# Routing six tiles ahead of the expert stream, 79 expert tiles per image instead of 80, and eleven output buffers

## The chip, the cores and the metric

The kernel runs on one core of one Trainium2 chip. The metric is the device time of one execution in microseconds. A core has TensorE (PE), VectorE (DVE), ScalarE (ACT), GpSimd (POOL) and SyncE (SP, which here only issues DMAs), each with its own in-order instruction stream; they meet at semaphores. SP, ACT and POOL start transfers, which 16 DMA engines carry out.

## The reference, cut to what matters

```python
# x: (2, 256, 96, 96)
x = x + conv_ref(_ln_c(x), ...)       # 4 dilated softmax branches, projection, group norm, relu
t = _to_tokens(x)                     # 2 * 9216 tokens of 256 channels
t = t + _L0_ffn_ref(_ln_t(t), ...)    # the mixture of experts below
x = _from_tokens(t, x)

def _moe(tokens, router_w, w1, b1, w2, b2):      # 8 experts, top 2
    probs = softmax(tokens @ router_w.T)
    rw, re = top_k(probs, 2);  rw = rw / rw.sum(-1)
    combine = zeros(N, 8).at[arange(N), re].set(rw)
    out = tokens
    for e in range(8):
        h = gelu(tokens @ w1[e] + b1[e], approximate=False)
        out = out + combine[:, e:e+1] * (h @ w2[e] + b2[e])
    return out
```

## The kernel before, in words

The program first does the convolution of image 0 and then that of image 1, up to about 1377 us. The routing of image 0 is done beside the convolution of image 1. What the change touches comes after it: the **expert stream**, which runs from 1377 us to 2145 us, and then the outputs of image 1.

**Expert tiles.** Each of an image's 9216 tokens goes to two experts, so there are 18,432 rows of 256 floats. The rows of one expert lie together in DRAM (`expert_in`), and the stream takes them 256 at a time. Each expert's last tile may be partly filled. `ETILES` is 18432 / 256 + 8 = 80 tiles per image, `STREAM` 160. For a tile SP loads `e_x` (`load_tile`, three buffers), PE turns it (`turn_in`), ACT and DVE split it (`e_hi`, `e_lo`), PE multiplies by the first weights (`first_product`, 12 matmuls), ACT applies gelu and splits (`hidden`, `e_act`, `h_hi`), DVE makes `h_lo`, PE multiplies by the second weights (`second_product`, 12 matmuls), DVE adds a bias into `e_out` (`output`), and POOL scatters `e_out` to DRAM (`expert_out`) by row indices with two indirect DMAs (`send`). `e_out` has `EO` = 4 buffers. Before the stream DMAs bring the first weights' second part (2.5 MB) and the second weights (`w2`, 4 MB).

**Routing of image 1.** It is interleaved with the stream of image 0. A tile iteration `n` has four ticks, `4n` to `4n + 3`; `routing(1, tick)` on each engine does what its `Schedule` has for that tick. A *slot* is one tile of 128 tokens: ACT loads blocks of two tiles (`load_block`) and applies relu (`relu_block`), DVE adds (`add_block`), PE turns the tile and makes the logits (`turn_tile`), ACT keeps them in `r_ln` (`keep_slot`), DVE takes the moments. Six slots are a *pair* (72 slots, 12 pairs). After a pair's last slot come its standard deviation, the choice of two experts in some twenty small DVE operations (`choose`), residual and normalisation of its six tiles, and, after ranking on PE at slot `RANK_AT`, the places of its rows (`place`). POOL then scatters them to `expert_in` with 12 indirect DMAs in three thirds of four (`scatter_rows`); `scatter_after` says behind which tile's `send` each third stands. `r_ln` has buffers for `HELD` = 3 pairs: ACT's first slot of pair p waits for the scatters of pair p - 3. Slots stand 3.5 ticks apart from tick 12 on, so 8 slots go with 7 tiles, from tile 3 to tile 65. After pair 11 DVE builds the tables of image 1 (`tables`); SP then writes fill rows behind each expert's rows (`fill_ends`, 8 DMAs at the first tile of image 1), waits for those and for all row scatters, and loads that tile.

**Outputs.** While the stream of image 1 runs, image 0 is finished in 24 groups of 384 tokens: ACT loads `o_y` (768 KB) and `o_acc` (384 KB), DVE weighs, PE turns, ACT copies and stores 384 KB. `out_group_at` puts one group on every third tile from tile 87 to 156. The 24 groups of image 1 follow after the stream.

## Time and profile before

| | us |
|---|---|
| median of three runs | 2252.12 (2251.94 to 2254.53) |
| the profiled execution, its own time | 2248.74 |
| span of its profile | 2246.9 |
| convolution, to | about 1377 |
| expert stream | 1377 to 2145 |
| outputs of image 1 | 2145 to 2247 |

| engine | busy us | share |
|---|---|---|
| PE | 1910.4 | 85% |
| DVE | 1560.9 | 69% |
| ACT | 1333.7 | 59% |
| POOL | 1083.1 | 48% |

The profiled execution took 3.4 us less than the median. Its own time is 1.8 us more than its span. Where this text says tile n it is the n-th expert tile from 0, and its time is the start of the DVE instruction that writes its `e_out`. The clock column is the TensorE clock granted, as a share of 2.4 GHz.

### The profile page before, as it was taken

To read this page: it belongs to the slowest core of one execution; us is meant where nothing else is said; L and a number is where in the kernel's file an instruction comes from. 1 tells how busy PE (TensorE), PEld (TensorE's weight loads), DVE (VectorE), ACT (ScalarE), POOL (GpSimd) and SP (SyncE) were. 2 spreads that over 40 slices of the span, in tenths; PEclk is the share of its full clock that TensorE was granted. 3 is DMA by queue.
4 is the path that set the end of the run, shared out by engine and by line. 5 is a ranking of instruction groups with operands and counts; after the bars stand their busy time and mean duration, and the time that the engine had idled before them with its cause. 6 is when DMAs were issued, how large, how long until landed. Compare 5 with 4: busy or idle time off the path is not lost.

```text
span 2246.9 us, 56560 instructions
## 1 busy us (share of the span) xinstructions
PE 1910.4 (85%) x20204; PEld 1832.1 (82%) x20204; DVE 1560.9 (69%) x4184; ACT 1333.7 (59%) x2877; POOL 1083.1 (48%) x1430
## 2 busy tenths in 40 slices
PE   5899799999969997999998895888888868999943
PEld 4899798999859997898888884888887768999932
DVE  4577675666556775777777774688887856777765
ACT  4677343333327774556556541887777758888822
POOL 3666212222215663145655562367777775555510
PEclk9999799999979998999999997898899989999965
DMA  4332597567554434677888879567667667888889
GB/s 143 105 106 78 145 294 189 141 173 174 153 142 133 132 102 111 190 228 216 227 232 245 237 209 322 171 219 227 224 218 225 202 192 274 284 282 283 280 310 368
DMA packets 341802, 459.87 MB, mean 205 GB/s; under 512 B 82677, under 2 KB 262709, under 8 KB 339173
## 3 DMA queue, kind: packets, MB, share of 16 engines
q1 hardware_dynamic: 231208, 246.52, 38.7%
q10 hardware_dynamic: 68433, 109.55, 14.9%
q0 software_dynamic: 41888, 100.18, 13.0%
q8 instruction: 168, 2.75, 0.5%
q14 instruction: 105, 0.86, 0.1%
HBM read 291.86 MB, written 174.69 MB: 208 GB/s over the span
## 4 chain that ended last, share of the span: by engine, by line
PE 46%; ACT 14%; DVE 13%; POOL 9%; issue 7%; DMA 7%; ACTq 3%; SPq 1%; POOLq 1%; DVEq 1%
PE ps_y L424 17%; PE ps_a L424 7%; PE ps_o L1050 6%; PE ps_b L987 4%; POOL expert_in L2148 4%; PE ps L424 3%; ACT w_now L1494 3%; POOL expert_out L2224 3%; ACT e_act L1483 3%; DMA o_acc<-res_scratch 3%; PE ps_tok L897 1%; DVE cat_lo L1938 1%; PE ps_o L1037 1%; ACT h_hi L1486 1%; DMA y_scratch<-y_acc 1%
## 5 line engine op out<-in xcount | busy, mean ns | idle before, releaser
L424 PE MATMUL ps_y<-cat_hi,wp 128*128 128x288 f32 x2048 | 483.5, 312 | 1.8 <-DVE cat_lo L1938 1.8
L2224 POOL DMA_INDIRECT expert_out<-e_out,e_dest x320 | 327.4, 1023 | 248.2 <-DVE e_out L2048 177.2
L2202 POOL DMA_DIRECT2D patches<-rows_scratch x340 | 190.4, 604 | 499.3 <-PE ps_o L1037 301.4
L424 PEld LDWEIGHTS ps_y<-cat_hi,wp 128*128 128x128 f32 x2048 | 354.4, 195 | 2.0 <-DVE cat_lo L1938 2.0
L2148 POOL DMA_INDIRECT expert_in<-r_ln,r_pos x288 | 290.0, 1007 | 106.3 <-issue 86.3
L2168 POOL TENSOR_TENSOR taps<-taps,g_rows 96x108 f32<-96x108 f32 (+2 forms) x416 | 243.8, 611 | 162.5 <-ACT g_rows L1310 158.6
L1379 ACT ACTIVATE bands<-ps_b 112x288 f16<-112x288 f32 (+4 forms) x256 | 105.1, 411 | 345.4 <-PE ps_b L987 331.9
L424 PE MATMUL ps_y<-cat_lo,wp 128*128 128x288 f32 x1024 | 308.1, 301 | 0.0
L424 PE MATMUL ps<-w,h_hi 128*128 x1280 | 258.5, 301 | 53.9 <-DVE h_lo L2037 51.1
L1938 DVE SCALAR_TENSOR_TENSOR cat_lo<-ps_o,cat_hi 128x288 fp32r<-128x288 f32 (+1 forms) x576 | 228.2, 419 | 92.9 <-ACT cat_hi L1385 89.4
L424 PE MATMUL ps<-e_hi,w_now 128*128 128x256 f32 x1280 | 266.1, 292 | 4.8 <-ACT w_now L1494 2.1
L1385 ACT ACTIVATE cat_hi<-ps_o 128x288 fp32r<-128x288 f32 (+1 forms) x576 | 211.9, 384 | 97.5 <-PE ps_o L1037 49.6
L424 PEld LDWEIGHTS ps<-w,h_hi 128*128 128x128 f32 x1280 | 206.0, 199 | 68.7 <-issue 68.2
L1930 DVE SCALAR_TENSOR_TENSOR bands<-ps_b,bands 112x288 f16<-112x288 f32 (+4 forms) x256 | 116.5, 455 | 189.1 <-ACT bands L1379 182.3
L1050 PE MATMUL ps_o<-bands,patches 112*128 112x72 f16 (+2 forms) x4608 | 198.4, 201 | 40.3 <-DVE cat_lo L1938 24.9
L424 PEld LDWEIGHTS ps<-e_hi,w_now 128*128 128x128 f32 x1280 | 218.1, 199 | 6.4 <-issue 4.0
L1050 PEld LDWEIGHTS ps_o<-bands,patches 112*128 112x128 f16 (+2 forms) x4608 | 176.9, 102 | 48.0 <-issue 46.5
L424 PEld LDWEIGHTS ps_y<-cat_lo,wp 128*128 128x128 f32 x1024 | 200.0, 195 | 0.0
L1483 ACT ACTIVATE e_act<-ps,b_of 128x256 f32<-128x256 f32 x320 | 133.9, 471 | 109.5 <-PE ps L424 70.6
L424 PE MATMUL ps_a<-wg,xc_hi 128*96 128x324 f32 x768 | 180.1, 320 | 11.6 <-DVE xc_lo L1902 11.6
L424 PE MATMUL ps<-e_lo,w_now 128*128 128x256 f32 x640 | 184.6, 288 | 0.0
L424 PE MATMUL ps<-w,h_lo 128*128 x640 | 184.4, 288 | 0.0
(201 smaller groups left out, 4488.3 us busy)
## 6 DMA issues: line engine op xcount, KB each, us to landing
e_x<-expert_in SPq DMA_DIRECT2D x160, 260.0 KB
patches<-rows_scratch SPq DMA_DIRECT2D x160, 192.0 KB
patches<-rows_scratch SPq DMA_DIRECT2D x256, 108.0 KB
patches<-rows_scratch SPq DMA_DIRECT2D x204, 112.0 KB
x_in<-in_x SPq DMA_DIRECT2D x48, 384.0 KB, 3.7
rows_scratch<-rows_st SPq DMA_DIRECT2D x48, 384.0 KB, 4.2
r_x<-in_x ACTq DMA_DIRECT2D x72, 256.0 KB
r_y<-y_scratch ACTq DMA_DIRECT2D x72, 256.0 KB
```

What stands on the lines that cost most here:

```text
L424: mm = eng.matmul(out, lhs[p], rhs[q], start=start and n == 0, stop=stop and n == 2)
L987: return pe.matmul(out, sel[:, b, 3 * y + x], pixels, start=True, stop=True, skip_group_check=True)
L1050: mm = pe.matmul(out, ring[:, (2 * p + z) * C + c * 128:(2 * p + z) * C + (c + 1) * 128], band_of[:, q, p * 72:(p + 1) * 72], start=k == 0 ...
L1379: act.activation(bands[0:k, s % 2, 0, first:first + n], ps_b[0:k, 0:n], ACT.Relu).then_inc(band_hi_done, 1)
L1385: act.activation(cat_pixels(cat_hi[:, s % 2, c], s, j), out_pixels(ps_o[:, n % 2], s), ACT.Copy, scale=UNSCALE).then_inc(cat_hi_done, 1)
L1483: last = act.activation(e_act[:, u, f], ps_1[:, u, f], ACT.Gelu, bias=b1_of[:, r, f, i:i + 1])
L1930: dve.scalar_tensor_tensor(out=bands[0:k, s % 2, 1, first:first + n], in0=ps_b[0:k, 0:n], scalar=0.0, in1=bands[0:k, s % 2, 0, first:first ...
L1938: dve.scalar_tensor_tensor(out=cat_pixels(cat_lo[:, s % 2, c], s, j), in0=out_pixels(ps_o[:, n % 2], s), scalar=UNSCALE, in1=cat_pixels(ca ...
L2148: pool.indirect_dma_start(out=xs_dram, out_offset=bass.IndirectOffsetOnAxis(ap=r_pos[:, p % HELD, z, t:t + 1], axis=0), in_=r_ln[:, p % HE ...
L2168: last = pool.tensor_tensor(here, here, g_rows[:, u, first:end, i, b:b + nb].rearrange("p r b k -> p r (b k)"), ALU.add)
L2202: pool.dma_start(patch_target(s, n), patch_source(m, s, n)).then_inc(patch_pooled[s % RING], 16)
L2224: pool.indirect_dma_start(out=ys_dram, out_offset=bass.IndirectOffsetOnAxis(ap=e_dest[:, i, j:j + 1], axis=0), in_=e_out[:, u, j], in_offs ...
```

## The change

One expert tile per image is left out: 7 experts at most can have a partly filled tile beyond 72 full ones, so 79 always suffice. `ETABLE` keeps 80 entries in the tables, `ETILES` is 79, `STREAM` 158. Then: slots stand 4 ticks apart and begin at tick -24, so that six slots are done before tile 0 and one goes with each tile up to 65; the group norm of image 1 stands ahead of them, and the load of `w2` behind the first two block loads; `group_factors(1)` and the first two `add_block` of DVE move ahead in the same way. `e_out` gets seven more buffers (`e_more`), in a ring of eleven up to tile 142 (`SHORT` = 143) and of four after it. Row scatters stand up to five tiles earlier in POOL's stream than the slots' plan alone would have them. Output groups stand 2.65 tiles apart, from tile 93 to 154. `send(n)` now waits for the scatters of tile n - 4.

```diff
-ETILES = PIX * TOP // S + E
+ETABLE = PIX * TOP // S + E
+ETILES = ETABLE - 1
+EO_MORE = 7
...
-        RANK_AT = TP + 4
-        SLOTS = RANK_AT + TP * (CPAIRS - 1) + 1
+        RANK_AT = (TP + 4, TP + 2)
+        SLOTS = [at_ + TP * (CPAIRS - 1) + 1 for at_ in RANK_AT]
+        AHEAD = 24
-        expert_ticks = [4 * 3 + (7 * k_ + 1) // 2 for k_ in range(SLOTS)]
+        expert_ticks = [4 * k_ - AHEAD for k_ in range(SLOTS[1])]
...
-        OUT_FIRST = ETILES + 7
+        OUT_RING = EO + EO_MORE
+        SHORT = (STREAM - 2 * EARLY - 4) // OUT_RING * OUT_RING
+        def out_buffer(n):
+            u = n % OUT_RING if n < SHORT else (n - SHORT) % EO
+            return e_out[:, u] if u < EO else e_more[:, u - EO]
+        def out_user_before(n):
+            return n - OUT_RING if n < SHORT + EO else n - EO
+        def sent_through(n):
+            return 16 * (S // 128) * (n // EO + 1)
+        OUT_FIRST = ETILES + 14
+        OUT_LAST = STREAM - 4
+        out_tile = {OUT_FIRST + g_ * (OUT_LAST - OUT_FIRST) // (GROUPS_OUT - 1): g_ for g_ in range(GROUPS_OUT)}
...
+            pe.wait_ge(r_kept, slots_before(1, 0))
+            group_sums(1, ps_g)
             turn_in(0)
             turn_in(1)
+            for u in range(-AHEAD, 0):
+                routing(1, u)
...
-            act.wait_ge(tabled, TABLE_ALL)
-            input_hi(0)
-            input_hi(1)
-            act.wait_ge(w_loaded_1, 32)
-            weights_hi(0)
-            weights_hi(1)
+            group_deviation(1)
             act.wait_ge(y_stored, 16 * (24 + 18))
             act.wait_ge(y_pooled, 16 * 6)
             for j in range(RY):
                 load_block(BLOCKS + j)
+            act.dma_start(w2[:].rearrange("p e z c -> p (e z c)").bitcast(F32), w_dram[1].rearrange("p e z c -> p (e z c)")).then_inc(w_loaded_2, 16)
+            act.wait_ge(tabled, TABLE_ALL)
+            input_hi(0)
+            input_hi(1)
+            act.wait_ge(gn_dve, 18)
+            for j in range(RY):
+                relu_block(BLOCKS + j)
+            load_block(BLOCKS + RY)
+            for u in range(-AHEAD, 0):
+                routing(1, u)
+            act.wait_ge(w_loaded_1, 32)
+            weights_hi(0)
+            weights_hi(1)
...
-                after(dve, e_scattered[n % EO], 16 * (S // 128) * (n // EO))
+                used = out_user_before(n)
+                if used >= 0:
+                    dve.wait_ge(e_scattered[used % EO], sent_through(used))
...
             def send(n):
+                if n >= EO:
+                    pool.wait_ge(e_scattered[u], sent_through(n - EO))
                 pool.wait_ge(e_out_done, n + 1)
...
             def scatter_after(p, q):
-                return plans[1].placed(p) // 4 - 1 + q
+                return plans[1].placed(p) // 4 - 1 + q - (OUT_RING - EO - 1) * p // CPAIRS
```

How ACT's stream reads from the load of the first weights' second part on (`w` is either weights tile, 128x8192 is `w2`), first before:

```order
L1468 DMA w<-expert_weights 128x5120 [waits proj_done]
L1470 DMA w<-expert_weights 128x8192
L1475 ACTIVATE e_hi<-ps_x 128x512 [waits e_turned,tabled]
L1475 ACTIVATE e_hi<-ps_x 128x512 [waits e_turned]
L1492 TENSOR_LOAD etable [waits w_loaded_1]
L1492 ISA x2
L1494 ISA
L1494 ACTIVATE w_now<-w 128x1024
```

and then the same place of the changed kernel:

```order
L1497 DMA w<-expert_weights 128x5120 [waits proj_done]
L1231 ACTIVATE gn_tmp<-gn_tmp,eps 128x2 [waits gn_dve]
L1239 DMA r_x<-in_x 128x2x256 [waits r_tok,r_x1,y_pooled,y_stored]
L1240 DMA r_y<-y_scratch 128x2x256
L1239 DMA r_x<-in_x 128x2x256 [waits r_x1,r_tok]
L1240 DMA r_y<-y_scratch 128x2x256
L1563 DMA w<-expert_weights 128x8192
L1503 ACTIVATE e_hi<-ps_x 128x512 [waits e_turned,tabled]
L1503 ACTIVATE e_hi<-ps_x 128x512 [waits e_turned]
L1247 ACTIVATE r_y<-r_y,gn_bias,gn_scale 128x256 [waits r_loaded0,gn_dve]
```

The load of `w2` moved behind the wait for `y_stored` and two block loads, and in front of all later block loads.

POOL's stream at the end of the routing, first before (the last two pairs' thirds among the scatters of the tiles; x2 is one tile):

```order
L2148 DMA expert_in<-r_ln,r_pos 155648x260 x4
L2224 DMA expert_out<-e_out,e_dest 45056x256 x6
L2148 DMA expert_in<-r_ln,r_pos 155648x260 x4
L2224 DMA expert_out<-e_out,e_dest 45056x256 x2
L2148 DMA expert_in<-r_ln,r_pos 155648x260 x4
L2224 DMA expert_out<-e_out,e_dest 45056x256 x2
L2148 DMA expert_in<-r_ln,r_pos 155648x260 x4
L2224 DMA expert_out<-e_out,e_dest 45056x256 x176
```

and of the changed kernel:

```order
L2180 DMA expert_in<-r_ln,r_pos 155648x260 x4
L2258 DMA expert_out<-e_more,e_dest 45056x256 x8
L2180 DMA expert_in<-r_ln,r_pos 155648x260 x4
L2258 DMA expert_out<-e_more,e_dest 45056x256 x2
L2180 DMA expert_in<-r_ln,r_pos 155648x260 x4
L2258 DMA expert_out<-e_more,e_dest 45056x256 x2
L2180 DMA expert_in<-r_ln,r_pos 155648x260 x4
L2258 DMA expert_out<-e_out,e_dest 45056x256 x8
```

Before, 88 tiles' scatters stand behind the last row scatter, so 72 stand ahead of it. Now the last three thirds stand behind the scatters of tiles 63, 64 and 65, so 66 tiles stand ahead.

## Rows read from the trace of the kernel before

**Rows 1.** The page's first line.
```profile
span 2246.9 us, 56560 instructions
```

**Rows 2.** Windows: stretch, length, busy time of each engine, clock, DMA share, GB/s.
```profile
1377.00:1406.50 29.50, 2.23 (x8) 1.45 (x9) 8.19 (x19) 2.39 (x4) 5.39 (x6) 0.54 0.96 388
1406.50:1435.00 28.50, 24.48 (x170) 22.73 (x171) 17.72 (x40) 23.54 (x40) 6.18 (x6) 0.88 0.59 181
...
1480.00:1780.00 300.00, 249.66 (x1936) 239.53 (x1935) 249.73 (x790) 236.49 (x442) 229.91 (x225) 0.91 0.69 223
1780.00:1850.00 70.00, 48.43 (x366) 46.52 (x367) 44.39 (x112) 38.76 (x67) 54.04 (x53) 0.88 0.60 191
...
1900.00:2145.00 245.00, 233.91 (x1979) 227.57 (x1978) 184.48 (x394) 201.13 (x350) 134.46 (x134) 1.00 0.83 277
2145.00:2247.00 102.00, 36.51 (x144) 27.43 (x144) 59.46 (x145) 19.47 (x24) 3.19 (x4) 0.51 0.94 358
```

**Rows 3.** DMA issues from 1376 to 1420: kind, count, size, median us to landing.
```profile
w<-expert_weights ACTq DMA_DIRECT2D x1, 4096.0 KB, 25.4
...
y_scratch<-y_acc POOLq DMA_DIRECT2D x6, 384.0 KB, 22.9
...
b<-in_b ACTq DMA_DIRECT2D x1, 1024.0 KB, 6.8
```

**Rows 4.** Timeline of PE, the start: us, duration, line, tiles, idle before and releaser.
```profile
1397.38 1.11 PE L1113 MATMUL ps_x<-ident,e_x 128*128 128x128 f32 x4 [20.79 <-DMA e_x<-expert_in]
...
1406.51 0.55 PE L424 MATMUL ps<-e_hi,w_now 128*128 128x256 f32 x1 [2.12 <-ACT w_now L1494]
```

**Rows 5.** Timeline of DVE: the e_out of tiles 0, 65, 77, 83, 92, 159.
```profile
1421.82 0.69 DVE L2048 TENSOR_TENSOR e_out<-ps,b 128x512 f32<-128x512 f32 x1 [0.29 <-PE ps L424]
...
1777.43 0.69 DVE L2048 TENSOR_TENSOR e_out<-ps,b 128x512 f32<-128x512 f32 x1 [0.81 <-PE ps L424]
...
1843.09 0.68 DVE L2048 TENSOR_TENSOR e_out<-ps,b 128x512 f32<-128x512 f32 x1
...
1863.03 0.69 DVE L2048 TENSOR_TENSOR e_out<-ps,b 128x512 f32<-128x512 f32 x1
...
1899.98 0.68 DVE L2048 TENSOR_TENSOR e_out<-ps,b 128x512 f32<-128x512 f32 x1
...
2145.20 0.69 DVE L2048 TENSOR_TENSOR e_out<-ps,b 128x512 f32<-128x512 f32 x1 [1.23 <-PE ps L424]
```

**Rows 6.** Groups by line, POOL, 1480 to 1780.
```profile
L2148 POOL DMA_INDIRECT expert_in<-r_ln,r_pos x120 | 121.3, 1011 | 36.6 <-issue 36.6
...
L2224 POOL DMA_INDIRECT expert_out<-e_out,e_dest x105 | 108.9, 1037 | 33.6 <-issue 30.2 <-DVE e_out L2048 3.5
```

**Rows 7.** Groups by line, DVE, 1480 to 1780: the part of one routed tile.
```profile
L1632 DVE BATCH_NORM_STATS2 r_stats<-r_ln 128x6 f32<-128x256 f32 x60 | 25.0, 417 | 0.0
...
L1634 DVE BATCH_NORM_AGGREGATE r_mv<-r_stats 128x2 f32<-128x6 f32 x60 | 10.9, 182 | 2.1
...
L1624 DVE TENSOR_TENSOR r_x<-r_x,r_y 128x512 f32<-128x512 f32 x28 | 19.1, 683 | 0.0
```

**Rows 8.** Waits: ACT from 1480 to 1780, then DVE from 1800 to 1850.
```profile
ACT r_ln L1231 <- DMA expert_in<-r_ln,r_pos: 9.7, 3, 5.8
...
DVE e_out L2048 <- DMA expert_out<-e_out,e_dest: 20.1, 6, 6.5
```

**Rows 9.** Timeline of SP, POOL and PE, 1813 to 1839: the hand-over.
```profile
1813.79 10.50 SPq L780 DMA_DIRECT2D expert_in<-in_k_fill  x8
...
1831.78 0.96 POOL L2148 DMA_INDIRECT expert_in<-r_ln,r_pos  x1 [0.30 <-issue]
...
1838.03 1.11 PE L1113 MATMUL ps_x<-ident,e_x 128*128 128x128 f32 x4 [8.13 <-DMA e_x<-expert_in]
```

**Rows 10.** From 1900 to 2100: waits of PE, groups of POOL.
```profile
PE ps_x L1113 <- DMA e_x<-expert_in: 0.3, 1, 0.3
...
L2224 POOL DMA_INDIRECT expert_out<-e_out,e_dest x107 | 108.0, 1009 | 92.2 <-DVE e_out L2048 73.1 <-issue 19.1
```

More of the change, by code:

```diff
@@ L322, in build @@
         o_out = sbuf(ctx, "o_out", [128, 2, CC, TC])
+        with ExitStack() as r1:
+            e_more = sbuf(r1, "e_more", [128, EO_MORE, S // 128, C])
         res_early = sbuf(ctx, "res_early", [128, EARLY, TT, C])
@@ L529, in __init__ @@
                 self.pair_end = {self.ticks[TP * p + TP - 1]: p for p in range(CPAIRS)}
-                self.pair_rank = {self.ticks[TP * p + RANK_AT]: p for p in range(CPAIRS)}
+                self.pair_rank = {self.ticks[TP * p + rank_at]: p for p in range(CPAIRS)}
             def kept(self, p, h):
@@ L535, in placed, with ranked_in @@
             def placed(self, p):
-                return max(self.ticks[TP * p + RANK_AT] + 4, self.ticks[TP * p + TP - 1] + 17)
-        plans = (Schedule(conv_ticks, (-2, 2), (-1, 1)), Schedule(expert_ticks, (-3, 1), (-3, 3)))
-        def ranked_in(k):
-            return (k - RANK_AT) // TP if k >= RANK_AT and (k - RANK_AT) % TP == 0 else None
+                return max(self.ticks[TP * p + self.rank_at] + 4, self.ticks[TP * p + TP - 1] + 17)
+        plans = (Schedule(conv_ticks, RANK_AT[0], (-2, 2), (-1, 1)), Schedule(expert_ticks, RANK_AT[1], (-3, 1), (-3, 3)))
+        def ranked_in(r, k):
+            return (k - RANK_AT[r]) // TP if k >= RANK_AT[r] and (k - RANK_AT[r]) % TP == 0 else None
         def slots_before(r, k):
-            return r * SLOTS_KEPT + sum(i < ITILES or ranked_in(i) is not None for i in range(k))
-        SLOTS_KEPT = sum(i < ITILES or ranked_in(i) is not None for i in range(SLOTS))
+            kept_in = lambda q, end: sum(i < ITILES or ranked_in(q, i) is not None for i in range(end))
+            return sum(kept_in(q, SLOTS[q]) for q in range(r)) + (kept_in(r, k) if k else 0)
         ALL_PAIRS, ALL_BLOCKS = IMAGES * CPAIRS, IMAGES * BLOCKS
@@ L563, in out_loads, with sent_all @@
             return 16 * sum(1 if early(k) else 2 for k in range(g % OB, g + 1, OB))
-        OUT_FIRST = ETILES + 7
+        OUT_RING = EO + EO_MORE
[10 more added lines that the diff above has]
+        out_tile = {OUT_FIRST + g_ * (OUT_LAST - OUT_FIRST) // (GROUPS_OUT - 1): g_ for g_ in range(GROUPS_OUT)}
         GATE_AT = 20
         def out_group_at(n):
-            g = (n - OUT_FIRST) // 3
-            return g if n >= OUT_FIRST and (n - OUT_FIRST) % 3 == 0 and g < GROUPS_OUT else None
+            return out_tile.get(n)
+        def sent_all(u, tiles):
+            return 16 * (S // 128) * len(range(u, tiles, EO))
         def halves(s):
@@ L818, in _ @@
                 if n == STREAM - 2 * EARLY:
+                    for u in range(EO):
+                        sp.wait_ge(e_scattered[u], sent_all(u, SHORT))
                     for u in range(2):
@@ L1572, in _ @@
                     write_out(g)
-                if n >= OUT_FIRST - 3 and sent < GROUPS_OUT and sent <= (n - OUT_FIRST + 3) // 3 + OB - 2:
+                begun = sum(n_ <= n + 3 for n_ in out_tile)
+                if n >= OUT_FIRST - 3 and sent < GROUPS_OUT and sent <= begun + OB - 3:
                     load_outputs(sent)
@@ L2101, in _ @@
             dve.memset(r_ln[:, 1, :, MARK:XC], 0.0)
-            group_factors(1, ps_g)
+            for j in range(RY):
+                add_block(BLOCKS + j)
+            for u in range(-AHEAD, 0):
+                routing(1, u)
             for n in range(STREAM):
                 hidden_lo(n)
-                if n == 2:
-                    add_block(BLOCKS)
-                    add_block(BLOCKS + 1)
                 routing(1, 4 * n)
@@ L2239, in _ @@
             for u in range(EO):
-                pool.wait_ge(e_scattered[u], 16 * (S // 128) * STREAM // EO)
+                pool.wait_ge(e_scattered[u], sent_all(u, STREAM))
 _INS = [
```

71 lines of the change are left out of this document (30 added, 41 removed).

## The prediction

> **What bounds the kernel now.** I read the windows first. Up to 1377 us nothing is changed. Between 1377 and 1406.5 us PE works 2.23 of 29.5 us, while the DMA engines are 96% busy: the machine waits for weights, for y_scratch and for the first expert tiles [rows 2 to 4]. From 1480 to 1780 us, tiles with routing, no engine is full: PE 83%, DVE 83%, ACT 79%, all in one chain from tile to tile. POOL is the exception. Its 225 scatters have 230 us of busy time, and 66.8 us of "issue" lie between them; together that is 1.333 us per scatter, and it waited only 3.5 us for e_out [rows 2, 6]. So POOL is just as fast as the tiles. What this costs stands in the waits: 9.7 us of ACT on r_ln (three pairs of rows held), and after 1800 us, 20.1 us of DVE on the four e_out buffers, when POOL had fallen behind [rows 8]. At the hand-over to image 1 the last row scatter starts at 1831.78 us, and PE had stood still for 8.13 us when tile 80 arrived at 1838.03 us [rows 9]. After that PE is 95% busy at full clock (1900 to 2145 us), and the outputs of image 1 end the span in 102 us on DMA engines 94% busy [rows 2].
>
> **The tiles' own pace.** From tile 77 to 83, without routing or outputs, 19.94 us for 6 tiles: 3.3 us [rows 5]. From tile 0 to 65: 355.6 us, of which 65 x 3.3 = 214.5 are the tiles, 9.7 the r_ln waits, and 131.4 the routing. That is 72 slots and the later work of 11 pairs. Of one pair I count 48% as slots: on DVE a slot is 0.417 + 0.182 + 0.683 / 2 = 0.94 us [rows 7], 5.6 for six, about half of what a pair costs. So 131.4 / (12 x 0.48 + 11 x 0.52) = 11.45 us per pair.
>
> **The change, part by part.**
>
> 1. Start. Before, the first product is at 1406.51 us and tile 0 is out at 1421.82 [rows 4, 5]. Now blocks must come first. Their wait is y_scratch, 22.9 us to landing beside the weights' loads [rows 3]. With w2's 4 MB moved behind them I take 10 to 15 us less, about 1394; the same weight at 388 GB/s [rows 2] is 10.8 us. Two block loads, relu and add give slot 0 at about 1401. Block 2 is issued behind w2 on ACT's queue and I take it to land at 1409; then four slots, with relu and loads of blocks 3 and 4 in turn on ACT, give the end of slot 5 at about 1420, relu 4 and the first weights at 1424. The group norm lies in DMA time, free. First product 1424, tile 0 out 11 us later, since table loads and group norm no longer stand in it: **1435, +13 us**. Bounds: 1425 if w2 does not delay block 2 and y_scratch is early; 1462 if each of five block loads took the 6.8 us of the bias load [rows 3] on the path.
>
> 2. Tiles 0 to 65. 66 slots are left in place of 72, so 11 slot parts and 11 later parts: 65 x 3.3 + 11 x 11.45 = 340.5 us, tile 65 at 1775.5, as before (1777.43 [rows 5]). Half a pair's work went to the start, the r_ln wait goes, since a pair's rows now leave four tiles before its buffer is wanted (before, under two).
>
> 3. Tiles 66 to 76. 11 x 3.3 + 6 us of pair 11 = 42.3: tile 76 at 1817.8. With eleven buffers the 20.1 us of DVE waits go [rows 8]. What is late next, three things:
>  - POOL: 66 tiles x 2 + 144 row scatters = 276 ahead of the last, against 288. It is continuous from tile 2 on (1445), so 272 x 1.333 = 363: 1808.
>  - the rows themselves: places of pair 11 at tile 69.25, about 1795; 16 scatters behind it, 21 us: 1816.
>  - SP's fills: issued when tile 76 has been taken, at about tile 72, 1775.5 + 6 x 3.3 + 6 + 3.3 = 1804.6, and 10.5 us long [rows 9]: 1815.
>  All three, with the 5.3 us that lay between the last row scatter's end (1832.74) and PE's first turn (1838.03) [rows 9], here 5.5, come to **1821.5** for the first tile of image 1, against 1838.03: **-16.5 us**. They lie within 13 us of each other, so a cheaper tile gains little more.
>
> 4. The rest. Before, 2145.20 - 1838.03 = 307.2 us for 82 iterations; now 81, without output work at 3.3 to 3.7 each: **-3.6 us**. One tile less in image 0 is already in 3.
>
> 5. Outputs of image 0: 24 groups over 61 tiles in place of 69. PE's and ACT's work per group is the same, so as a sum nothing. But bytes: 61 x 0.528 MB + 24 x 1.573 MB = 70.0 MB. Tiles 92 to 159 took 245.2 us [rows 5], 67 x 3.3 + 24 x 1.0, so this stage should now take 61 x 3.3 + 24 x 1.08 = 227 us: 308 GB/s, where 277 went at 83% busy [rows 2]. By that share it would be 92%. Between 0 (PE waited 0.3 us for e_x in 200 us [rows 10]) and 25.6 us (rival C) I take **+2**, near the row.
>
> 6. send's wait for tile n - 4: eight scatters, 10.7 us, lie between. Nothing; up to a few us if landing took as long. The tail is unchanged: 102 us.
>
> Sum: -16.5 - 3.6 + 2 = -18.1, where the +13 of the start lies inside the first term. Against the profiled execution (2248.74 us, 1.8 more than its span of 2246.9 [rows 1]) that is 2230.6. The median of the runs is 3.4 higher, so **2234 us**.
>
> **The skill on two places.** In rows 6 a scatter takes 1011 and 1037 ns with DVE 83% busy, in rows 10 1009 ns at 75%. The Trainium skill, SBUF — State Buffer, "SBUF: two separate sides", says that GpSimd cannot write descriptors while DVE runs an operation on both ports; its part "A bandwidth-pool intuition that's wrong" gives about 3.1 us in place of 0.62 for such a DMA. If each scatter were held like that, 272 of them would be an estimated 843 us; the trace bears out hardly 30 ns, so the sum goes by 1.333. The second is block 2 behind w2: rows 3 show 25.4 us for w2 behind another load, and nothing here shows two loads overtaking. The Trainium skill, DMA: Bandwidth & Descriptors, "Queues, rings and completion order", says descriptors of one issuer are taken in ring order; that speaks against the change, and by it the block waits for all of w2; without it the start would be 5 us earlier.
>
> **Rivals.**
>
> A. Faster. Routing laid at one slot per tile costs a pair 9 us, since bursts no longer meet two slots. Tile 76 would be at 1791, but POOL's 1808 and the 5.5 us hold: 1813.5, 8 less: 2226; with the start 8 us early as well 2218. For it: DVE has 17% idle in small waits. Against: the chain, not the load, makes the pace.
>
> B. POOL still the bound. At 1.40 us per scatter it ends at 1826, tile 79 at 1831.5, ten more: 2244. For it: single scatters of 1.4 to 1.6 us lie in the trace's mean of 1037 ns; against: that mean.
>
> C. Slower: the DMA engines bound the stage with image 0's outputs. At the 277 GB/s of rows 2, 70.0 MB take 252.7 us instead of 227: 2234 - 2 + 25.6 = 2257.6, slower. It decides from 278 GB/s downward. For it: 8% to 11% more bytes per time, a tile load only three deep, share 83% already. Against: 358 GB/s in the last window, and PE never waited.
>
> D. The ring and the order buy nothing, because the tiles' chain takes back what the waits leave: -3.6 and the start half repaid, 2250.
>
> **How the numbers follow.** Forecast 0.45 (own range 2224 to 2245), A 0.23, B 0.11, C 0.13, D 0.08. A measurement of this kernel tells 0.2%, 4.5 us: same is 2247.6 to 2256.6. Faster: forecast, A and nearly all of B, 0.78. Same: D and the edge of B, 0.09. Slower: C, 0.13. The range leaves out A's better half and C's worse: 2212 to 2256.
>
> **What would show it.** The first product near 1424 and tile 0 near 1435; ACT waiting once for r_x or r_y of block 2. No ACT wait on expert_in, no DVE wait on expert_out up to tile 76. Tile 65 within 5 us of 1776. Row scatters ending near 1816, and SP's fills ending at about the same time. The stage with outputs at about 305 GB/s and PE's waits for e_x under 5 us. I am wrong if tile 0 is past 1445, if a pair costs over 12.5 us, or if PE waits for e_x among the outputs.

## The result, and the profile after

The changed kernel took 2259.11 us median of 20 runs (2249.64 to 2267.75), the kernel before beside it 2251.19 (20 runs, 2240.59 to 2256.63); the ratio is 1.0046, 95% interval 1.0034 to 1.0058. It is slower by about 0.46%, where the forecast of 2234 us stood for a gain of 0.8%. The profiled executions are 2263.68 and 2248.74 us: 14.9 us apart, while the medians are 7.9 apart, since one lies above its median and the other below. To read the numbers further on: in the three first and in the last session of experiments the kernel before itself took 2524 to 2544 us, in another 2248; chip 15 showed both levels, so each kernel is compared only with what ran beside it.

The page's first line, against [rows 1]:

```profile
span 2261.8 us, 56526 instructions
```

The windows of the changed kernel, against [rows 2] (same columns):

```profile
1377.00:1406.50 29.50, 6.80 (x36) 5.62 (x36) 12.87 (x32) 2.35 (x5) 5.41 (x6) 0.60 0.87 320
1406.50:1435.00 28.50, 9.97 (x45) 9.47 (x46) 10.68 (x23) 8.71 (x17) 0.00 (x0) 0.50 0.69 253
1480.00:1780.00 300.00, 248.70 (x1986) 242.76 (x1986) 249.46 (x758) 238.27 (x443) 219.89 (x219) 0.90 0.68 218
1780.00:1850.00 70.00, 52.28 (x389) 50.37 (x388) 51.40 (x132) 42.04 (x72) 52.66 (x52) 0.86 0.62 199
1900.00:2145.00 245.00, 226.46 (x1903) 221.35 (x1901) 183.94 (x391) 198.30 (x338) 133.40 (x127) 0.99 0.87 295
```

The second line shows the later start: from 1406.5 to 1435 us PE was busy 9.97 us where it had been 24.48. Among the tiles, from 1480 to 1780 us, no engine is fuller than before. The stages, from the starts of DVE's `e_out` instructions and PE's last convolution product (us; "start" is from that product to tile 0, T is 79, before 80):

| | conv. end | start | tiles 0-65 | 65 to image 1's first | its tile 0 to 14 | 14 to last | after it | span |
|---|---|---|---|---|---|---|---|---|
| before | 1376.6 | 45.2 | 355.6 | 75.9 | 55.7 | 236.2 | 101.7 | 2246.9 |
| after | 1380.4 | 70.8 | 342.6 | 67.3 | 50.5 | 245.5 | 104.6 | 2261.8 |

**The start.** Timelines of the changed kernel; first ACT and DVE:

```profile
1401.24 0.39 ACTq L1239 DMA_DIRECT2D r_x<-in_x  x1
...
1405.14 1.08 ACT L1247 ACTIVATE r_y<-r_y,gn_bias,gn_scale 128x256 f32<-128x256 f32 x2
...
1406.26 0.82 DVE L1824 TENSOR_TENSOR bias_parts<-erank,order 128x640 f32<-128x640 f32 x1
...
1410.58 0.66 DVE L1653 TENSOR_TENSOR r_x<-r_x,r_y 128x512 f32<-128x512 f32 x1
...
1422.19 0.60 ACT L1247 ACTIVATE r_y<-r_y,gn_bias,gn_scale 128x256 f32<-128x256 f32 x1 [7.26 <-DMA r_y<-y_scratch]
```

then PE (the second of its lines begins tile 0's second product), against [rows 4], and DVE, with tiles 0 and 65, against [rows 5]:

```profile
1411.38 0.66 PE L874 MATMUL ps_k<-ident,r_x 128*128 128x128 f32 x2 [12.51 <-DVE r_x L1653]
...
1433.04 0.55 PE L428 MATMUL ps<-e_hi,w_now 128*128 128x256 f32 x1 [4.21 <-ACT w_now L1522]
...
1441.79 0.49 PE L428 MATMUL ps<-w,h_hi 128*128 x2
...
1447.36 0.21 DVE L1715 TENSOR_TENSOR r_either<-r_chosen 128x48 f16<-128x48 f32 x1
...
1451.23 0.69 DVE L2080 TENSOR_TENSOR e_out<-ps,b 128x512 f32<-128x512 f32 x1 [0.63 <-issue]
...
1793.80 0.69 DVE L2080 TENSOR_TENSOR e_more<-ps,b 128x512 f32<-128x512 f32 x1 [0.69 <-issue]
```

`y_scratch` was complete at 1401.2, when ACT issued the first block. Slot 0 then waited for `add_block`, which stood on DVE behind five instructions of `first_biases` (4.3 us); block 2, issued behind `w2` on ACT's queue at 1411.33, let ACT wait 7.26 us. PE had the second product of tile 0 done at about 1443.4 us, but its `e_out` stands in DVE's stream behind the choice of pair 0 and other routing work, with which DVE was busy from 1441.2 to 1450.6 us without a pause.

**The tiles.** Waits of the changed kernel: PE and POOL from 1500 to 1800 us, then DVE's on the scatters from 1500 to 1850 (us in total, times, longest):

```profile
PE ps_k L884 <- DVE r_either L1715: 39.7, 10, 4.7
...
POOL expert_in L2180 <- DVE r_ln L1760: 15.9, 5, 5.9
...
DVE e_more L2080 <- DMA expert_out<-e_out,e_dest: 1.6, 2, 1.0
DVE e_more L2080 <- DMA expert_out<-e_more,e_dest: 1.3, 2, 0.7
```

The 20.1 us of DVE waits on the buffers and ACT's 9.7 us [rows 8] are gone. In their place are two that the kernel before did not have: PE stands in the ranking product for the choice of experts (ranking comes at slot TP + 2 instead of TP + 4), and POOL in the moved row scatters for rows not yet written.

POOL's groups of the changed kernel from 1480 to 1780 us, against [rows 6]:

```profile
L2180 POOL DMA_INDIRECT expert_in<-r_ln,r_pos x112 | 113.2, 1011 | 45.9 <-issue 30.6 <-DVE r_ln L1760 12.9 <-DVE e_more L2080 1.5
L2258 POOL DMA_INDIRECT expert_out<-e_more,e_dest x69 | 69.0, 1000 | 21.7 <-issue 20.4 <-DVE e_more L2080 0.9 <-DVE e_out L2080 0.3
L2258 POOL DMA_INDIRECT expert_out<-e_out,e_dest x38 | 37.7, 993 | 11.6 <-issue 11.3 <-DVE e_out L2080 0.3
```

219 scatters against 225: POOL did less per time, 12.9 us of it waiting for `r_ln`.

**The hand-over**, timeline of SP, POOL and PE, against [rows 9]:

```profile
1829.36 0.57 SPq L806 DMA_DIRECT2D expert_in<-in_k_fill  x1
...
1832.90 0.97 POOL L2180 DMA_INDIRECT expert_in<-r_ln,r_pos  x1 [0.30 <-issue]
...
1843.58 0.35 SPq L819 DMA_DIRECT2D e_x<-expert_in  x1
...
1846.15 1.11 PE L1141 MATMUL ps_x<-ident,e_x 128*128 128x128 f32 x4 [7.38 <-DMA e_x<-expert_in]
```

The last row scatter ends at 1833.87, 1.1 us later than before. SP's fills begin 15.6 us later than before, go on for 9.8 us, and only 4.4 us behind them is image 1's first tile loaded.

Which of the two was awaited last can be read from SP's waits from 1750 to 1850 us, first before, then changed (L783 is the wait for the row scatters, L817 the first instruction behind all waits of `fill_ends`):

```profile
SPq L783 <- DMA expert_in<-r_ln,r_pos: 10.0, 1, 10.0
...
SPq L817 <- DMA expert_in<-in_k_fill: 3.6, 1, 3.6
```

Before, SP waited 10.0 us for the row scatters and loaded 2.6 us behind the last one. In the changed kernel it waited for the fills, and the load came 9.7 us behind the last row scatter. The fills are issued when tile 72 is under way (its `e_out` is at 1828.1 us), so here the late tiles set the hand-over, and POOL's rows came second.

**The outputs**, waits of PE and SP from 1900 to 2150 us, against [rows 10]:

```profile
PE ps_x L1141 <- DMA e_x<-expert_in: 11.9, 6, 5.1
...
SPq L848 <- DMA expert_out<-e_more,e_dest: 9.1, 1, 9.1
```

L848 is SP's wait for all scatters up to tile `SHORT` - 1 = 142, just before it reuses `e_more`'s place for residuals; the tile loads are queued behind it, and PE starves 5.1 us.

### The profile page after: what moved, and what is told of

It is laid out like the page before. It is cut to its first block, busy times and chain, and to the rows that moved or that the text cites. A ratio compares the mean times of both kernels' runs of the same rounds, so it can differ in the third digit from the quotient of the medians.

```text
span 2261.8 us, 56526 instructions
## 1 busy us (share of the span) xinstructions
PE 1907.8 (84%) x20148; PEld 1836.5 (81%) x20148; DVE 1564.8 (69%) x4176; ACT 1331.4 (59%) x2865; POOL 1077.6 (48%) x1426
## 3 DMA queue, kind: packets, MB, share of 16 engines
q0 software_dynamic: 41696, 99.65, 12.8%
## 4 chain that ended last, share of the span: by engine, by line
PE 49%; DVE 20%; DMA 10%; ACT 8%; issue 6%; POOL 3%; DVEq 2%; ACTq 1%; SPq 1%; POOLq 1%
PE ps_y L428 17%; PE ps_a L428 7%; PE ps L428 6%; PE ps_o L1078 6%; PE ps_b L1015 4%; DMA out<-o_out 3%; DMA e_x<-expert_in 2%; DVE h_lo L2067 2%; PE ps_tok L925 2%; DVE e_lo L2057 1%; DVE cat_lo L1967 1%; ACT e_act L1511 1%; PE ps_o L1065 1%; DVEq L2073 1%; DVE r_x L1653 1%
## 5 line engine op out<-in xcount | busy, mean ns | idle before, releaser
L428 PE MATMUL ps<-w,h_hi 128*128 x1264 | 259.5, 304 | 31.3 <-DVE h_lo L2067 29.1
L428 PE MATMUL ps<-e_hi,w_now 128*128 128x256 f32 x1264 | 255.0, 286 | 5.4 <-ACT w_now L1522 4.2
L2258 POOL DMA_INDIRECT expert_out<-e_more,e_dest x182 | 184.5, 1014 | 100.1 <-DVE e_more L2080 52.4
L428 PEld LDWEIGHTS ps<-e_hi,w_now 128*128 128x128 f32 x1264 | 212.6, 197 | 6.0 <-issue 4.3
L2258 POOL DMA_INDIRECT expert_out<-e_out,e_dest x134 | 138.7, 1035 | 148.0 <-DVE e_out L2080 113.8
```

The source lines that it names most:

```text
L428: mm = eng.matmul(out, lhs[p], rhs[q], start=start and n == 0, stop=stop and n == 2)
L2258: pool.indirect_dma_start(out=ys_dram, out_offset=bass.IndirectOffsetOnAxis(ap=e_dest[:, i, j:j + 1], axis=0), in_=out_buffer(n)[:, j], in ...
```

## Experiments

Columns as above; "ratio" is to the kernel before in the same session, with its 95% interval. e1 to e4 ran in one session and e5, the changed kernel again, in the next, together with e6 to e8; a stage of e1 to e4 is compared with e5's across the two. By the ratio e1, e3 and e4 lie within e5's interval, so what is read from them is the stage alone. At the slower level:

| | start | 0-65 | 65-img1 | 0-14 | 14-last | after | ratio |
|---|---|---|---|---|---|---|---|
| f1 before, again | 44.0 | 478.8 | 94.0 | 56.0 | 247.9 | 102.9 | 0.9999 (0.997-1.0029) |
| e5 changed | 69.4 | 546.2 | 92.5 | 52.5 | 253.6 | 103.2 | 1.0372 (1.03-1.0444) |
| e1 w2 last | 61.8 | 543.1 | 91.0 | 54.7 | 255.2 | 103.2 | 1.0325 (1.0292-1.0358) |
| e2 TP + 3 | 68.7 | 506.4 | 100.6 | 54.0 | 256.1 | 102.9 | 1.024 (1.0201-1.0279) |
| e3 SHORT 132 | 69.2 | 544.6 | 89.4 | 54.0 | 246.4 | 103.4 | 1.0332 (1.0296-1.0369) |
| e4 every 3rd | 68.9 | 550.1 | 90.2 | 58.5 | 254.6 | 102.5 | 1.0357 (1.032-1.0394) |
| e6 e1+e2+e3 | 63.0 | 513.6 | 100.4 | 54.8 | 246.1 | 103.1 | 1.0223 (1.0154-1.0291) |
| e7 none ahead | 43.0 | 499.4 | 111.8 | 54.4 | 255.7 | 102.9 | 1.0162 (1.0095-1.0229) |
| e8 TP + 4 | 69.0 | 470.8 | 104.1 | 53.6 | 253.0 | 102.9 | 1.0121 (1.0055-1.0187) |
| f2 four edits | 59.5 | 473.1 | 104.1 | 53.5 | 243.3 | 104.4 | 1.009 (1.0056-1.0124) |
| f3 and no shift | 59.9 | 456.4 | 89.5 | 55.4 | 245.4 | 102.3 | 0.9972 (0.9946-0.9998) |
| f4 ring, none ahead | 42.9 | 468.1 | 89.2 | 54.6 | 249.5 | 103.1 | 0.9962 (0.9936-0.9988) |
| h1 as f2 | 59.7 | 473.5 | 105.2 | 55.5 | 243.7 | 104.6 | 1.0084 (1.0056-1.0113) |
| h2 12 ahead | 50.8 | 523.2 | 86.8 | 53.9 | 248.8 | 102.9 | 1.0118 (1.0079-1.0156) |

At the level of the prediction (before: 2248.17 us, 29 runs):

| | start | 0-65 | 65-img1 | 0-14 | 14-last | after | median | ratio |
|---|---|---|---|---|---|---|---|---|
| g1 no shift only | 69.5 | 340.3 | 68.2 | 50.4 | 245.5 | 103.5 | 2259.04 | 1.0045 (1.0032-1.0058) |
| g2 12 ahead | 51.6 | 354.4 | 68.0 | 50.7 | 243.8 | 103.2 | 2246.16 | 0.9988 (0.9974-1.0003) |
| g3 24 ahead | 60.1 | 335.2 | 77.7 | 51.8 | 237.5 | 102.3 | 2248.38 | 1.0002 (0.9987-1.0017) |
| g4 no ring | 45.6 | 355.7 | 76.5 | 50.2 | 241.9 | 102.5 | 2250.55 | 1.001 (0.9997-1.0023) |

**e1, `w2` behind the slots.**

```diff
-            act.dma_start(w2[...] ...)      # behind the first two load_block
             for u in range(-AHEAD, 0):
                 routing(1, u)
+            act.dma_start(w2[...] ...)
             act.wait_ge(w_loaded_1, 32)
```

> The changed kernel with one edit: ACT issues the load of w2 (4 MB) after the six slots of the start instead of before the load of block 2. Theory S (the start eats the gain: in the changed kernel the first product came 52.6 us after the last projection, 29.9 before, and ACT waited 7.3 us for block 2 behind w2): the first product comes 5 to 8 us earlier (about 46 us), tile 0 follows 18 us behind it, and the run is 5 to 8 us faster than the changed kernel. Rival (hand-over fixed by something else, so that an earlier start is given back): first product earlier, but tile 65 to image 1's first tile (67.3 us) grows by as much and the time stays within 2 us. A second way to miss: w2 now lands after tile 0 needs it, then PE waits before the first second product and tile 0 comes over 22 us after the first product.

The start is 7.6 us shorter than e5's (51.2 to 43.6 us up to the first product), the rest as it was. ACT's wait for block 2, 7.26 us in the changed kernel, was `w2` ahead of it on the queue.

**e2, ranking one slot later**, and **e8, two slots later** (as before).

```diff
-        RANK_AT = (TP + 4, TP + 2)
+        RANK_AT = (TP + 4, TP + 3)          # e8: TP + 4
```

> The changed kernel with one edit: the ranking of a pair on PE one slot (four ticks) later, RANK_AT TP + 3 in place of TP + 2. In the changed kernel PE waited 39.7 us in ten ranks for r_either (end of the choice on DVE) from 1500 to 1800 us; before there was no such wait. Theory R (that wait is on the chain between tiles): the wait falls under 5 us and tiles 0 to 65 take 342.6 - 20 to 35 = 308 to 322 us; the hand-over then eats some of it, the run is 10 to 20 us faster. Rival (DVE is what the chain goes through; PE only waits somewhere else): the wait moves to h_lo and tiles 0 to 65 stay within 5 us of 342.6, the run within 3 us.

> The changed kernel with the ranking two slots later, as before (TP + 4). Theory R: no PE wait for r_either; tiles 0 to 65 the same as with one slot later (which on the slow chip gave 506 in place of 545 us), but pair 11 is placed a tile later and the hand-over grows by 3 to 5 us: 8 to 20 us faster than the changed kernel. Rival: tiles 0 to 65 within 5 us of the changed kernel.

Tiles 0 to 65 take 506 and 471 us instead of 546; 8 and 12 us are given back at the hand-over. The direction is as theory R had it, at a level where everything is longer. PE's waits for `r_either` were only 9.6 us in e5 from 1580 to 2000 us, so they are not the 75 us. At this level much of the time among the tiles goes into waits that nothing in the profile ends ("remote"): ACT's on `e_act` alone are 150.9 us between tiles 0 and 65 of e5 and 100.8 us in e8. What an edit saves there through the order of the work, and what through fewer of these waits, stays open.

**e3, the ring's last lap left out.**

```diff
-        SHORT = (STREAM - 2 * EARLY - 4) // OUT_RING * OUT_RING
+        SHORT = (STREAM - 2 * EARLY - 4) // OUT_RING * OUT_RING - OUT_RING
```

> The changed kernel with one edit: the ring of eleven output buffers ends one round earlier, SHORT 132 in place of 143. In the changed kernel SP waited 9.1 us at tile 148 for the scatters through tile 142 before it could overwrite e_more with res_early, and PE then waited 5.1 us for e_x, with a gap of 9.8 us between two tiles. Theory B (a new wait of the ring's end): SP's wait goes, PE's e_x wait goes, the stage from tile 93 to the last is 4 to 7 us shorter (245.5 to 240), the run 4 to 7 us faster. Rival (DMA engines are full there anyway): the stage stays within 2 us.

The output stage is 7.2 us shorter than e5's. SP's waits from 2100 us on had this row in e5, and none for this line in e3:

```profile
SPq L848 <- DMA expert_out<-e_more,e_dest: 8.7, 1, 8.7
```

**e4, output groups every third tile from tile 85.**

```diff
-        OUT_FIRST = ETILES + 14
+        OUT_FIRST = ETILES + 6
-        out_tile = {OUT_FIRST + g_ * (OUT_LAST - OUT_FIRST) // (GROUPS_OUT - 1): g_ ...}
+        out_tile = {OUT_FIRST + 3 * g_: g_ for g_ in range(GROUPS_OUT)}
```

> The changed kernel with one edit: the output groups of image 0 on every third tile from tile 85 on (to tile 154), as dense as before, in place of 2.65 tiles apart from tile 93. Theory C (rival C of the prediction: denser groups make the DMA engines the bound): from image 1's first tile to the last tile 296.0 us falls by 5 to 10 and the run is 5 to 10 us faster. Rival (groups cost the same wherever they stand): the sum stays within 2 us, or grows by some us because ACT's first load now waits for POOL to have sent all of image 0.

Image 1's tiles take 313.1 us in place of 306.1: more, not less. The closer groups had cost nothing, and rival C is out.

**e5, the changed kernel; e6, e1 to e3 together; e7, routing and start as before.**

> The changed kernel unchanged, as the measure for the runs beside it on the same chip. The first four runs were on a chip on which the kernel before took 2544 us, with hundreds of 1 to 3 us in which PE waited for nothing that the profile shows. If that chip is met again: ratio to before 1.03 to 1.035, tiles 0 to 65 about 545 us. On an ordinary one: ratio 1.003 to 1.006, start 52 us, tiles 0 to 65 343 us.

> The changed kernel with the three edits together: w2 loaded after the six slots, ranking one slot later, ring ended at tile 132. Theories S, R and B add: start 7 us less, tiles 0 to 65 15 to 35 us less of which 0 to 10 come back at the hand-over, the output stage 6 to 9 less: 25 to 40 us faster than the changed kernel, ratio to before 0.985 to 0.995 on an ordinary chip. Rival (POOL and the hand-over take the gain of the ranking back): only start and ring remain, 12 to 16 us.

> The changed kernel with routing as before (slots from tile 3 on, 3.5 ticks apart, ranking at TP + 4, the order of the start as before, w2 early), so that 79 tiles, the ring of eleven, the earlier row scatters and the output groups remain. Theory S+R (what was lost lies in the routing ahead): start 29.9 us as before, tile 65 to image 1 55 to 65 in place of 75.9, output stage as in the changed kernel: ratio to before 0.990 to 0.998. Rival (the ring and the order of scatters cost themselves, since each send waits for an older one): 1.000 or above.

e5 loses 3.7% where the same program lost 0.46%. e6 adds the parts up (start -6.4, tiles -32.6, outputs -7.5 against e5). e7 was the surprise: without any routing ahead it still loses 1.6%, so at this level the loss could not be the start and the rank alone. What it still had in common with the changed kernel was the shift of the row scatters, the ring, the 79 tiles, the wait of `send` and the places of the output groups.

**f1 to f4: the shift.** f2 is the changed kernel with e8, e1, e3 and `add_block` ahead of `first_biases` on DVE; f3 the same without the shift; f4 is e7 with e3 and without the shift; f1 the kernel before.

```diff
-                return plans[1].placed(p) // 4 - 1 + q - (OUT_RING - EO - 1) * p // CPAIRS
+                return plans[1].placed(p) // 4 - 1 + q          # f3, f4
```

> The kernel before, unchanged, for its own trace on the same chip as the three that follow. On the first chip it took 2251 us with tiles 0 to 65 in 355.6 us; on the two chips of the earlier experiments it took 2524 and 2544 us. Theory 1 (such a chip adds stalls of engines of 5 to 20 us that no semaphore ends, and spreads them over the whole kernel): on such a chip tiles 0 to 65 take 440 to 480 us here, and the output stage after image 1's 15th tile about 250. Theory 2 (the extra time on such a chip hits only the changed kernels): 360 to 400 us.

> The changed kernel with four edits: pairs ranked TP+4 slots after their start in image 1 too (as before), w2's load after the six slots of the start, the two added blocks ahead of the first bias sums on DVE, and SHORT 132 instead of 143. Theory R+S+B (rank, w2's place and the last eleven-buffer lap are the three costs): start (last convolution product to first expert product) 40 us or less against 52.6; the output stage 7 us shorter; on a chip where before takes 2250 us, 2225 to 2240 us, below before by 0.5% to 1.1%; on a slower chip within 1% of before. Rival (the routing ahead costs by itself, whatever the rank): start 42 to 45, and slower than before by 0.3% or more.

> As the one before it, with the row scatters left at the tiles where the kernel before had them (without the shift by up to six tiles). Theory P (the shift lets POOL wait for rows that are not there yet, with outputs queued behind): tiles 0 to 65 as short or shorter, POOL's waits on r_pos and r_ln go from over 20 us to under 10, and the total is 0 to 10 us less. Rival (the shift carries the hand-over): from tile 65 to image 1's first tile 6 to 9 us more, total 6 to 9 us more.

> The kernel before's start and routing places, its scatter places, with 79 tiles per image, the eleven buffers with SHORT 132, the send's wait and the output groups spread out. Theory (79 tiles and the ring gain by themselves what the DVE waits on expert_out were): 15 to 25 us below before, so a ratio of 0.990 to 0.993. Rival (the ring changes nothing that is not taken back): within 5 us of before; if it is above 1.005, the spread of the output groups or the send's wait costs.

f3 is 26 us faster than f2 by that one edit. The waits of f2 from 1580 to 2000 us:

```profile
POOL expert_in L2180 <- DVE r_pos L1747: 45.0, 6, 12.1
...
DVE e_more L2080 <- remote: 45.1, 6, 11.6
```

and of f3:

```profile
DVE e_more L2080 <- remote: 0.5, 1, 0.5
```

POOL has no wait on `r_pos` in f3. It is tempting to join the two 45 us: POOL waits for rows, the outputs behind it are not sent, and eleven tiles on DVE waits for a buffer. The trace of f2 does not bear this out:

```profile
1920.49 0.69 DVE L2080 TENSOR_TENSOR e_more<-ps,b 128x512 f32<-128x512 f32 x1 [9.28 <-remote]
...
1936.36 0.97 POOL L2180 DMA_INDIRECT expert_in<-r_ln,r_pos  x1 [12.13 <-DVE r_pos L1747]
```

The first line is tile 48, which takes the buffer of tile 37. POOL had issued the last scatter of tile 37 by 1838.5 us, and by 1905.1 us it had landed, for there `send(45)` went on, whose wait counts it in; DVE's wait began at 1911.2. So the buffer was free. In the same time PE stood three times for 1.7 to 2.4 us between its matmuls with nothing that ends these waits, and POOL's wait for `r_pos` begins only behind DVE's. That the one edit is worth 1% at this level is shown (f2 against f3, and h1, which repeats f2); by what path is not: the hand-over has 14.6 us of it, the tiles 16.7, and ACT's "remote" waits on `e_act` between tiles 0 and 65 are 113.5 us in f2 and 62.9 in f3. f3's rival, that the shift carries the hand-over, falls here (89.5 us without it, 104.1 with it). f4 is the fastest kernel at this level (0.9962), f3 beside it.

**g1 to g4, at the level of the prediction.** g1 is the changed kernel without the shift, g3 is f3 again, g2 is g3 with these two lines, g4 is f4 with `SHORT` = 0, so four buffers:

```diff
-        AHEAD = 24
+        AHEAD = 12
-        expert_ticks = [4 * k_ - AHEAD for k_ in range(SLOTS[1])]
+        expert_ticks = [15 * k_ // 4 - AHEAD for k_ in range(SLOTS[1])]
```

> The changed kernel with one edit: the row scatters keep the tile numbers of the kernel before (no shift by up to six tiles). Theory P (a shifted scatter waits on POOL for rows not yet placed, and the outputs queued behind it hold e_out back): POOL's waits on r_ln (15.9 us in 1440 to 1800 us on the first chip, 66.1 us on a slower one) fall below 5, DVE's waits on e_more with no releaser go, and tiles 0 to 65 are shorter: 3 to 10 us on a chip where before takes 2250 us, 30 to 90 us on one where it takes 2530 (546 us there). Rival theory R (only the rank at TP+2 costs): tiles 0 to 65 within 5 us of the changed kernel's, the total within 5 us of it, or 6 more if the hand-over is late.

> The four edits and the scatters at their old tiles (the kernel that took 0.997 of before), with 12 ticks of routing ahead of the tiles instead of 24, at 3.75 ticks per slot instead of 4: three or four slots before tile 0 and the last at the same tick. Theory (each slot ahead costs PE about 1.5 to 2.5 us and gives back less among the tiles): the start is 5 to 8 us shorter, tiles 0 to 65 up to 3 longer, total 3 to 5 us below the kernel with 24. Rival (the start is bounded by block loads and not by slots): start the same within 2 us, total the same within 3.

> The kernel that took 0.997 of before on the third chip (pairs ranked at TP+4, w2 after the slots, block additions ahead of the bias sums, SHORT 132, scatters at their old tiles), again, beside the others of this call. On a chip of before's 2530 us: 0.994 to 1.000. On one of 2250 us: start 41 against 52.6, output stage 7 us shorter, PE's 39.7 us of waits on r_either gone, some 12 to 20 us of them off the span: 2225 to 2238 us, a ratio of 0.989 to 0.994. Rival: those waits were beside other waits, and it is 2240 to 2250.

> The kernel before's start, routing places and scatter places, four buffers everywhere, 79 tiles per image, the send's wait and the spread output groups; no buffer of the ring is used. It tells what the ring gives. Theory (79 tiles bring 2 x 3.3 to 3.6 us and the ring brings the DVE waits on expert_out, 20 us on the first chip): 3 to 10 us below before, and 8 to 20 us above the same kernel with the ring on a chip of 2250 us; on one of 2530 us, where POOL is not behind, ring or no ring within 5 us. Rival (the ring is worth nothing in either case): 0.996 of before, as with the ring.

g1 takes POOL's waits for `r_ln` away and changes the total by nothing (2259.04 us in its session, 2259.11 in the first; 1.0045 and 1.0046 of the kernel before). g3 takes PE's waits for `r_either`, the 10.7 us of the start and the 8.0 us of the outputs away, and gives 10.4 us back at the hand-over: 1.0002. Its rival is what came (2240 to 2250). In g4 DVE's waits on four buffers are back (15.5 us), and yet it is within 0.1% of the kernel before and of g3, and its hand-over takes 1.2 us less than g3's. The same program with the ring (f4) did not run at this level, so what the ring alone is worth here is not shown. Waits of g3, PE from 1440 to 1850 us and POOL from 1500 to 1830:

```profile
PE ps_x L1141 <- DMA e_x<-expert_in: 23.2, 1, 23.2
...
POOL expert_out L2258 <- DVE e_more L2080: 3.6, 9, 1.2
POOL expert_out L2258 <- DVE e_out L2080: 2.1, 7, 0.3
```

PE stands once, 23.2 us, at the hand-over, and POOL hardly waits at all. The timeline of g3 there:

```profile
1807.23 1.86 SPq L806 DMA_DIRECT2D expert_in<-in_k_fill  x2
...
1830.75 0.97 POOL L2180 DMA_INDIRECT expert_in<-r_ln,r_pos  x1 [0.30 <-issue]
...
1834.26 0.35 SPq L819 DMA_DIRECT2D e_x<-expert_in  x1
...
1837.08 1.12 PE L1141 MATMUL ps_x<-ident,e_x 128*128 128x128 f32 x4 [23.19 <-DMA e_x<-expert_in]
```

The fills are early, the rows last: here, unlike in the changed kernel, POOL's stream sets the hand-over. Counted in each trace from POOL's first output scatter to the end of the last row scatter (waits are those over 0.5 us; "per scatter" is the stretch less the waits, divided; beside it the end of SP's last fill and the start of SP's load of image 1's first tile):

| | first output | scatters | waits | per scatter | last row | last fill | load |
|---|---|---|---|---|---|---|---|
| before | 1422.8 | 288 | 28.7 | 1.324 | 1832.7 | 1824.3 | 1835.3 |
| after | 1452.2 | 276 | 22.8 | 1.300 | 1833.9 | 1839.1 | 1843.6 |
| g1 | 1444.2 | 286 | 12.7 | 1.300 | 1828.8 | 1828.8 | 1833.6 |
| g2 | 1420.7 | 286 | 24.6 | 1.319 | 1822.6 | 1814.3 | 1825.2 |
| g3 | 1440.8 | 290 | 10.0 | 1.313 | 1831.7 | 1817.1 | 1834.3 |
| g4 | 1422.5 | 288 | 32.9 | 1.313 | 1833.5 | 1822.9 | 1835.9 |

Six orders of the work, and the last row scatter ends within 12 us in all, within about 5 us without g2, whose convolution ended 8 us early. Where the rows come last (before, g2, g3, g4) the load follows them by 2.4 to 2.6 us. Where the fills come last, it follows the fills by 4.4 us in the changed kernel; in g1 both end together and it is 4.8 us. g3 has tile 65 18.8 us earlier than the changed kernel, and its load only 9.3 us earlier: with the fills out of the way, the rows were next.

**h1 and h2: the shift put back** into g3 and g2 (h1 is f2's program).

> The kernel of the last call that took 1.0002 of before (TP+4, w2 after the slots, block additions first, SHORT 132, 24 ticks ahead), with one difference: the row scatters are moved ahead by up to six tiles again, as in the changed kernel. Theory Q (POOL's rate of 1.333 us per scatter is what sets the hand-over: without the shift 290 scatters lie up to the last row scatter, from tile 0 at 1439.9 to 1831.7 us, and POOL waited 5.7 us in 330): with ten scatters fewer ahead of it the last one ends 1815 to 1821 us, PE's wait for e_x of 23 us at the hand-over falls to 7 to 12, and the total is 10 to 15 us less: 2233 to 2238 us, a ratio of 0.993 to 0.996. Rival W (POOL then waits for rows not yet placed, as in the changed kernel, 15.9 us, and on the slower chips 45 us): the last row scatter at 1828 or later and the total within 4 us of 2248. On a chip of 2530 us both expect W: 1.009.

> The same move of the row scatters, in the kernel with 12 ticks ahead and 3.75 ticks per slot (0.9988 of before). Theory Q: there POOL's last row scatter ended 1822.6 us in a run whose convolution ended 8 us early; with ten scatters fewer ahead it is 13 us earlier and PE's wait for e_x, 15.2 us, falls to 4 or less: 2234 to 2240 us, 0.992 to 0.996. Rival W: total within 4 us of 2246. If both kernels land at the same time, routing ahead by 24 or 12 ticks is worth the same, and the hand-over is POOL's alone.

Both ran at the slower level. h1 repeats f2: 1.0084 beside 1.009, POOL waiting 44.8 us for `r_pos`. h2's tiles 0 to 65, with slots 3.75 ticks apart, took 523 us against h1's 473. Whether ten scatters fewer ahead of the last row would free 10 us at the level of 2250 us wasn't seen.

## Why the prediction was wrong

The forecast span was 2228.8 us, the measured one 2261.8: 33.0 us more. By the steps, each apart from what it inherits: convolution's end +3.4 (unchanged code), first product +5.6, from there to tile 0 +7.2, tiles 0 to 65 +2.1, to PE's first turn of image 1 +6.3, its tiles +5.4, the last stage +2.9; together 32.9.

1. **Start: wrong by 12.8 us.** Predicted 1424 and 1435, measured 1433.0 and 1451.2. I took `y_scratch` at 1394 and slot 0 at 1401; it was complete at 1401.2 (the convolution had ended 3.4 us late), and slot 0 began at 1411.4, since I had left `first_biases`, 4.3 us on DVE, out of its path. Block 2 behind `w2` landed at about 1422, not 1409: the queue was right, its length was not; e1 has 7.6 us of it. The slots and the first weights behind it were shorter than I had them (11 us instead of 15), so only 9 us reach the first product. The 11 us from first product to tile 0 were 18.2: ACT's three table loads of 1.28 us, which I took to be gone, still stand there (from 1436.03 on), and DVE puts the choice of pair 0 and other routing ahead of tile 0's `e_out`, 9.4 us without a pause. PE's wait of 2.9 us for that choice is not the cause: g3, which ranks later and has no such wait, took 18.2 us as well.

   The Trainium skill, DMA: Bandwidth & Descriptors, "Queues, rings and completion order", says descriptors of one issuer are taken in ring order. The trace agrees: `w2`, issued at 1403.44, landed 16.5 us later, and only then block 2's 512 KB, 10.9 us after their issue at 1411.33. In g3, where `w2` is issued after the six slots, the loads of the blocks landed after 2.9 and 3.3 us (median).

2. **Tiles 0 to 65: right in size (342.6 against 340.5), for the wrong reason.** PE's 39.7 us of waits for `r_either`, from the earlier ranking, were not in the sum, and a slot on a fixed place in every tile is cheaper than I had it: g3, ranked at TP + 4, took 335.2. That the two nearly cancel is luck. g2, with slots 3.75 ticks apart and 68 of them among the tiles instead of 66, took 354.4, nearly as long as before did with 3.5. That fits one half of rival A (bursts don't meet).

3. **The hand-over: the step that failed.** I had PE's first turn of image 1 at 1821.5, 16.5 us earlier than before; it was at 1846.15, 8.1 us later. Of its three conditions I expected the rows themselves last, at 1816, the fills at 1815 and POOL's stream at 1808. The rows' own readiness, at 1816, bound nothing: POOL's last wait for `r_ln` ended at 1781.8. The other two came late.
   - The fills ended it. Predicted from 1804.6 to 1815, they ran from 1829.4 to 1839.1: tile 65 was 18.3 us late (convolution, start and item 2), and from there to the first fill it took 6.5 us more than the 29.1 that I had. From the last fill to PE's turn it was another 7.0 us, of which SP's wait for the landing has 3.6, and I had allowed 5.5.
   - POOL alone would have taken the gain as well: with the 2.4 to 2.6 us that lie behind the last row elsewhere, the load would have come at about 1836.4 (an estimate), not before the 1835.3 of the kernel before. I had its end at 1808, from tile 0 at 1435 and with no waits. It was 1833.9: 7.2 us because POOL's stream began at 1452.2 and not at 1445, 22.8 us of waits, 15.9 of them in the moved scatters for `r_ln`, less 3.8 for 276 scatters at 1.300 in place of 272 at 1.333. Against before: +29.4 for the start, -15.7 for 12 scatters fewer at 1.31, -5.9 waits, -6.6 by the rate: +1.2, measured 1.1.

   Of the 24.6 us between forecast and measurement 12.8 are the start's, 3.4 the convolution's, 2.1 those of item 2, and 6.3 the hand-over's own. Rival B (POOL the bound) describes the kernel before, g2, g3 and g4, where the load waits for the rows, and not the changed kernel; its rate of 1.40 was reached in none of the six traces above (1.300 to 1.324).

4. **The rest, outputs:** predicted 305.6 us from PE's first turn to the last tile, measured 311.0. SP's wait at `SHORT` 143 accounts for it (7.2 us less with 132 in e3 against e5, 8.0 in g3 against the changed kernel), which neither the forecast nor a rival had: the ring's end is a wait, and the tile loads stand behind it. Without it the stage would have taken about 303 to 304 us, an estimate from these two differences.

5. **Rival C** gave 2257.6, close to the time measured, by luck, for a reason that isn't there: 295 GB/s passed from 1900 to 2145 us, above its 277, and spreading the groups (e4) made it longer.

6. The send's wait cost nothing visible, as predicted: POOL's outputs waited for DVE and issue alone. The tail was 104.6, predicted 102.

Two of the signs named for being wrong came: tile 0 was past 1445 (1451.2), and PE waited 11.9 us for `e_x` among the outputs. A pair did not cost over 12.5 us: by the same reckoning (342.6 - 214.5) / 11 is 11.6.
